# Reordered preparation, halved expert loads, single-chunk weight loads and later zeros in a two-layer gated cross-attention kernel

## The reference, cut to what matters

```python
x = x + jnp.tanh(g_xattn[0]) * _L0_xattn_ref(ctx_1024, _layernorm(x, axis=-1), mask, ...)   # 8 heads
x = x + jnp.tanh(g_ffn[0])   * _L0_ffn_ref(_layernorm(x, axis=-1), gate_w, w1, w2, w3)      # 8 experts, top 2
x = x + jnp.tanh(g_xattn[1]) * _L1_xattn_ref(ctx_1024, _layernorm(x, axis=-1), mask, ...)   # 16 heads
x = x + jnp.tanh(g_ffn[1])   * _L1_ffn_ref(_layernorm(x, axis=-1), w1, conv_w, conv_b, w2)

# in the cross-attention of layer A
x = layernorm(x, gamma_media, beta_media)               # the context
latents = layernorm(latents, gamma_lat, beta_lat)       # the tokens
kv = jnp.concatenate((x, latents * kv_gate), axis=1)
q, k, v = latents @ Wq, kv @ Wk, kv @ Wv                # masked softmax over k, then @ Wout
```

## Time and profile before

| | us |
|---|---|
| median of 3 runs | 1506.27 |
| the runs | 1496.41 to 1508.53 |
| the profiled execution | 1507.64 |
| its span, first to last instruction | 1505.9 |

### The profile page before, as it was taken

The page is one execution under the profiler, slowest core; times in us unless marked ns, Lnnn a source line. Parts: engine busy times, 40 slices in busy tenths (PEclk is TensorE's granted clock), DMA queues, the critical chain, the costliest instruction groups (busy, mean ns, idle before and its releaser), DMA issues.

```text
span 1505.9 us, 44898 instructions
## 1 busy us (share of the span) xinstructions
PE 1252.2 (83%) x16822; PEld 980.5 (65%) x16822; DVE 1075.0 (71%) x2786; ACT 973.2 (65%) x2319; POOL 1116.6 (74%) x1359
## 2 busy tenths in 40 slices
PE   1868787768769898977999999899999999999842
PEld 0545565547658776655887887677777777777631
DVE  4868786876555556775666766688888888888744
ACT  2868785555545576654655555687888887787731
POOL 5869787686566675547676777789889888988754
PEclk9989998889999999987999999999999999999965
DMA  7499999886999974547999999544655455454520
GB/s 223 98 232 229 230 241 221 166 219 148 242 179 249 235 171 91 93 101 181 236 229 252 247 256 241 107 106 97 104 97 105 104 108 104 95 110 102 78 41 6
DMA packets 439336, 239.94 MB, mean 159 GB/s; under 512 B 388960, under 2 KB 420560, under 8 KB 430544
## 3 DMA queue, kind: packets, MB, share of 16 engines
q1 hardware_dynamic: 407496, 172.87, 56.6%
q10 hardware_dynamic: 28552, 56.86, 12.4%
q0 software_dynamic: 3072, 7.34, 1.8%
HBM read 107.78 MB, written 35.50 MB: 95 GB/s over the span
## 4 chain that ended last, share of the span: by engine, by line
PE 32%; POOL 23%; DMA 13%; DVE 10%; issue 7%; ACT 6%; SPq 4%; DVEq 2%; ACTq 1%; POOLq 0%
PE bank_ring L1089 6%; DMA probs_turned<-probs 6%; POOL probs L651 6%; DMA expert_up<-experts_up 6%; PE bank_ring L1075 5%; PE bank_ring L1127 5%; PE bank_scores L1049 4%; PE bank_out L1108 3%; POOL raw_weights L696 3%; PE bank_x L1188 2%; ACT scores L852 2%; PE bank_x L1141 2%; POOL raw_weights L697 2%; POOL affine L627 2%; SPq L521 2%
## 5 line engine op out<-in xcount | busy, mean ns | idle before, releaser
L651 POOL TENSOR_TENSOR probs<-scores,probs 112x487 f16<-112x487 f32 x384 | 425.9, 1126 | 223.1 <-ACT probs L859 218.3
L852 ACT ACTIVATE scores<-scores,score_min 112x487 f32<-112x487 f32 x384 | 265.5, 693 | 81.8 <-DVE score_min L1340 79.5
L1340 DVE CUSTOM_DVE_ANT_0 scores<-bank_scores,mask 112x487 f32<-112x487 f32 x384 | 239.1, 660 | 48.9 <-PE bank_scores L1049 43.8
L859 ACT ACTIVATE probs<-scores 112x487 f16<-112x487 f32 x384 | 214.7, 604 | 37.0 <-DMA probs_turned<-probs 21.8
L1089 PE MATMUL bank_ring<-weights,kv_B 128*128 128x128 f16 x3072 | 196.8, 222 | 1.8 <-DVE keys L1352 1.8
L1089 PEld LDWEIGHTS bank_ring<-weights,kv_B 128*128 128x128 f16 x3072 | 185.8, 99 | 11.1 <-DVE keys L1352 2.5
L1108 PE MATMUL bank_out<-values,probs_turned 128*128 128x64 f16 x4608 | 171.3, 194 | 23.3 <-DMA probs_turned<-probs 22.7
L1357 DVE SCALAR_TENSOR_TENSOR values<-bank_ring,values 128x512 f16<-128x512 f32 x192 | 131.2, 683 | 80.4 <-ACT values L879 80.4
L879 ACT ACTIVATE values<-bank_ring 128x512 f16<-128x512 f32 x192 | 112.6, 587 | 110.5 <-PE bank_out L1108 109.1
L1075 PE MATMUL bank_ring<-kv_B,weights 128*128 128x488 f16 x768 | 181.1, 372 | 0.0
L1108 PEld LDWEIGHTS bank_out<-values,probs_turned 128*128 128x128 f16 x4608 | 158.6, 99 | 26.7 <-DMA probs_turned<-probs 13.0
(11 more groups left out here) (230 smaller groups left out, 2474.8 us busy)
## 6 DMA issues: line engine op xcount, KB each, us to landing
expert_up<-experts_up SPq DMA_DIRECT2D x43, 1024.0 KB, 5.3
expert_down<-experts_down SPq DMA_DIRECT2D x43, 512.0 KB, 6.8
raw_weights<-in_weights ACTq DMA_DIRECT2D x8, 1536.0 KB, 11.1
experts_up<-expert_up ACTq DMA_DIRECT2D x8, 1024.0 KB, 4.8
raw_weights<-in_weights ACTq DMA_DIRECT2D x6, 1024.0 KB, 8.3
probs_turned<-probs SPq DMA_TRANSPOSE x384, 3.3
context_turned_B<-kv_B ACTq DMA_DIRECT2D x16, 375.0 KB, 9.1
kv_B<-context_turned_B ACTq DMA_DIRECT2D x16, 375.0 KB, 3.7
```

What stands on the lines that cost most here:

```text
L651: pool.tensor_tensor(PR[:, u % 4, 1, 0:KEYS], S[:, u % 4, 0:KEYS], PR[:, u % 4, 0, 0:KEYS], ALU.subtract).then_inc(probs_split, 1)
L852: act_e.activation(S[:, u % 4, 0:KEYS], S[:, u % 4, 0:KEYS], ACT.Exp, bias=rmin[:, u % 4:u % 4 + 1], scale=-1.0, accum_out=rsum[:, g % 2, ...
L859: act_e.activation(PR[:, u % 4, 0, 0:KEYS], S[:, u % 4, 0:KEYS], ACT.Copy).then_inc(probs_ready, 1)
L1340: dve.tensor_tensor_reduce(out=S[:, u % 4, 0:KEYS], in0=bS[u % 2][0:TOK, 0:KEYS], in1=mask[:, m, 0:KEYS], scale=1.0, scalar=3.0e38, op0=AL ...
```

## The change

1. Mask and latents. `make_mask` is a function of its own with a semaphore `mask_made`; for layer A, POOL makes the mask first thing in step 4n - 4, ahead of the contexts, and SP loads the mask's bytes a step earlier. The queries' latents (two L627s, one L631) are split in step 4n - 5, and ACT rounds them there. Step 4n - 3 keeps the keys' latents alone. Layer B keeps its order.
2. `rstd`: the product and the sum with eps leave POOL; DVE does them in one `tensor_scalar` after a drain behind the statistics (two `tensor_scalar`s for stage P). POOL keeps the power.
3. Tiles' first matrices: `up` in DRAM and SBUF is laid out in two halves of 512 KB, each with semaphores. Half 0 of tile i + 2 is loaded between the two turns of step i, half 1 of tile i + 1 where all of it was before. A load needs only its own half of the buffer to be free.
4. Layer B's attention weights: one DMA of 256 KB in each of steps 37 to 52, four steps before ACT rounds the chunk.
5. Zeros: batch 0's five DMAs one in a step from 27; batch 1's seven one in a step from 58, out of `eup`, which DVE clears in step 57.
6. DVE's order: in a step without a tile, `early` parts (outputs and routing inputs) go before `split_expert` and the quantisation; in a step with a tile, before the quantisation too.
7. `combine` and `stats("B")` of sequences 0 and 6 go to the end of DVE's step 58 and 106.

```diff
-ZERO_STEP, ZERO_EACH = 27, 2
+ZERO_STEPS = (27, 58)
...
+def load_up(b, i, half):
...
+    e = sp.value_load(ids[b][0:1, i:i + 1], min_val=0, max_val=EXPERTS - 1)
+    if t >= 2:
+        sp.wait_ge(up_ready, 2 * (t - 2) + half + 1)
+    sp.dma_start(eup[:, t % 2, HALF_WORDS * half:HALF_WORDS * (half + 1)], up_dram[e, half])
...
     if 2 <= i + 1 < TILES[b]:
-        load_expert(b, i + 1, 0)
+        load_up(b, i + 1, 1)
     if 2 <= i < TILES[b]:
-        load_expert(b, i, 1)
+        load_down(b, i)
...
-    for u in (2 * j, 2 * j + 1):
-        turn_probs(u)
+    turn_probs(2 * j)
+    for b in range(2):
+        if 2 <= j - first_tile_step(b) + 2 < TILES[b]:
+            load_up(b, j - first_tile_step(b) + 2, 0)
+    turn_probs(2 * j + 1)
...
 def rstd(stage, n, cols):
-    after(pool.tensor_tensor(r[:, 0:cols], m[:, 0:cols, 1], growth[:, 0:cols], ALU.mult))
-    after(pool.tensor_tensor(r[:, 0:cols], r[:, 0:cols], bias[:, 0:cols], ALU.add))
     pool.tensor_tensor(r[:, 0:cols], r[:, 0:cols], minus_half[:, 0:cols], ALU.pow)
...
 if (j + 4) % 4 == 0 and 0 < (j + 4) // 4 < NSEQ:
+    make_mask(0, (j + 4) // 4).then_inc(mask_made, 1)
     split_context((j + 4) // 4, 0, 0)
...
+if (j + 5) % 4 == 0 and 0 < (j + 5) // 4 < NSEQ:
+    split_query_latents((j + 5) // 4)
...
-if j in (FFN_STEP + 5, FFN_STEP + 9):
-    load_raw(12 + i, i, 4, weights_in, L1_AT + 4 * i)
-if j in (L1_STEP + 5, L1_STEP + 9):
-    load_raw(14 + i, i, 4, weights_in, L1_AT + 8 + 4 * i)
+c = j - L1_STEP + 4
+if 0 <= c < L1_CHUNKS:
+    act_e.wait_ge(ffn_rounded if c < 8 else l1_split, c % 8 + 1)
+    act_e.dma_start(raw4(c), weights_in[:, (L1_AT + c) * CHUNK:(L1_AT + c + 1) * CHUNK])
...
 def up(b, i, half):
+    pe.wait_ge(up_loaded[t % 2][half], 16 * (t // 2 + 1))
     if half == 0:
-        pe.wait_ge(up_loaded[t % 2], 16 * (t // 2 + 1))
         pe.wait_ge(xt_loaded[t % 2], 16 * (t // 2 + 1))
...
 def stats(stage, n):
     dve.bn_stats(bn[0:TOK, at, :], X[:, n])
     dve.drain()
-    dve.bn_aggr(mv[stage][0:TOK, 0, :], bn[0:TOK, at, :]).then_inc(stats_ready[stage], 1)
+    dve.bn_aggr(mv[stage][0:TOK, 0, :], bn[0:TOK, at, :])
+    dve.drain()
+    dve.tensor_scalar(rs[stage][0:TOK, 0:1], mv[stage][0:TOK, 0, 1:2], 1.0 + LN_EPS, LN_EPS * LN_EPS,
+                      ALU.mult, ALU.add).then_inc(stats_ready[stage], 1)
...
+def clear_expert():
+    dve.wait_ge(up_ready, 2 * TILES[0])
+    dve.memset(eup[:, 0, 0:ZERO_ROWS * 2 * DIM], 0.0).then_inc(eup_cleared, 1)
...
     for n in range(NSEQ):
-        if j == combine_step(n):
+        if j == combine_step(n) and n not in FIRST_OF_BATCH:
             combine(n)
...
+    for n in FIRST_OF_BATCH:
+        if j == combine_step(n):
+            combine(n)
+            stats("B", n)
```

More of the change, by code:

```diff
@@ L1703, in _ @@
                         f_scale(n, 1)
+                if m[0]:
+                    for c in l1_chunk(j - 1):
+                        split_l1_chunk(c)
+                    gate_hidden(m[0][1], m[0][2], m[0][3])
+                for t in early(j):
+                    part(t)
                 for c in expert_chunks(j - 1):
```

183 lines of the change are left out of this document (103 added, 80 removed).

## The result

| | us |
|---|---|
| changed kernel, median of 20 runs | 1508.31 |
| the runs | 1500.74 to 1514.36 |
| kernel before beside it, median of 20 runs | 1498.77 |
| ratio | 1.0055, 95% interval 1.0031 to 1.0080 |
| profiled span, changed kernel | 1506.7 |

1467 us was forecast; the change made the kernel half a per cent slower. Medians further down are of all runs of a kernel; ratios leave out the runs in a slower state that some executions fall into.

What follows compares the result with a forecast made beforehand. PE's gaps in layer A (DMA share 0.99, no engine full) and the tiles were taken to count, with later layer B PE-bound. Terms -1 - 6 - 4 - 2.5 - 18 - 7 - 4 + 2 + 1 - 0.5 = -40 took 1507.6 to 1467 us; range 1445 to 1490.

Steps and rivals of the forecast that it cites:

- The mask, the latents and eps (-6 and -2.5): Layer A: keys ready up to 3.1 us sooner, 6 us gained (0 to 12); steps 33 to 38: 2.5 us (1 to 4).
- Batch 0 (-18): Steps 43, 47, 51, 55: PE's gaps at half 0 shrink through halves and single chunks, 18 us gained (9.8 to 28).
- rival D: Tiles: halves do nothing since the rows decide; batch 0 gives 6, batch 1 nothing, 1487 us, chance 0.07.
- Batch 1 (-7): Batch 1's tiles: halves take nearly all of 8.6 us of PE's waits, 7 us gained (3 to 8.5).
- zeros (-4 in steps 27 to 32): Steps 27 to 32: 3.2 of 5.6 MB of zeros leave a full DMA stretch, 4 us gained (0 to 8).
- step 106 (-3): Step 106: combination moved last puts DVE's work ahead of its wait for the gather, 3 us gained.
- Zeros in layer B (+1): Steps 58 to 64: the zeros return where transfers are about half, 1 us lost; 8 if turns get late.
- combination in step 58 (-1): Step 58: combination moved last, with PE already ahead, 1 us gained.
- rival C: Steps 58 to 64: later zeros hold up layer B's first turns, seven waits of 49 us in all, 1516 us, chance 0.04.
- Eps in layer B (+2): Layer B: DVE's added eps operation and drain lengthen ten statistics steps where PE waits, 2 us lost (0 to 4).
- A: Rival: DMA engines full in steps 6 to 32, so gaps move instead of going; 1486 us, chance 0.17.
- signs of being right: PE's `expert_up` waits under 10 us, POOL waits 10 to 14, steps 27 to 32 51 us, steps 64 to 192 outside tiles unchanged.

Runs made afterwards that it cites:

- e14: Changed kernel with POOL's split of the queries' latents in step 4n - 4, behind the first half of the context: 1489.88 us, 0.9894 of the kernel before.
- e2: Changed kernel with edit 1 alone undone: 1481.62 us, 0.9896 of the kernel before.
- e13: Kernel before with ACT's part of edit 1 alone (queries' latents rounded in step 4n - 5, ahead of the contexts): 1521.05 us, 1.0109.
- e8: Changed kernel without edits 1 and 4 (layer B's weights in four 1 MB loads again): 1494.84 us, 0.9950 of the kernel before.
- e9: Changed kernel without edits 1 and 3 (whole first matrices, single chunks kept): 1493.67 us, 0.9985 of the kernel before.
- the six and the fourteen: Six profiles of the kernel before, alone or with parts of edit 1, and fourteen of the changed kernel or variants; steps 39 to 56: medians 205.9 and 183.8 us.
- e6: Changed kernel without edits 1 and 7 (first combinations in their old place): 1496.70 us, 0.9895 of the kernel before.
- e5: Changed kernel without edit 1, with batch 1's zeros begun in step 60 instead of 58: 1483.81 us, 0.9839 of the kernel before.
- e11: Changed kernel without edits 1 and 2 (eps back on POOL): 1476.93 us, 0.9884 of the kernel before.
- e18: Changed kernel without edit 1, later zeros begun in step 60, in more rounds: 1476.66 us, 0.9829 of the kernel before.
- e4: Changed kernel with DVE's order in a step as before: 1503.57 us, 1.0030 of the kernel before.
- e10: Kernel before with edit 1 alone, but POOL's split of the queries' latents behind the second split of the probabilities: 1532.35 us, 1.0219.
- e17: Changed kernel without edit 1, with half of each 1.5 MB experts' load in steps 5 to 20 left out: 1474.59 us, 0.9796 of the kernel before.
- e16: Changed kernel with half of each 1.5 MB experts' load in steps 5 to 20 left out: 1490.05 us, 0.9917 of the kernel before.

## Why the prediction was wrong

**The mask, the latents and eps (-6 and -2.5): the step that failed.** The prediction put together what edit 1 takes "out of step 4n - 3 ahead of the mask's semaphore", and did not ask what the moved piece waits for at its new place nor what is queued behind it there. Its two L631 operations and L634 stand in step 4n - 5 ahead of both splits of the probabilities, and L634 waits for a rounding that ACT does after its work on the probabilities and the values. What was removed was seen rightly: PE's wait for POOL fell from 28.9 us to 12.0 in the changed kernel (9.9 for L658 and 2.1 for the mask, inside the forecast's 10 to 14). What the removal brought can't be told from nothing: e14 has the same fall without the new wait, and its ratio is e2's, with 11 us of room either way. The unseen wait of POOL for ACT, 65.0 us in 13 places, made edit 1 as a whole a loss of 1.6%, some 24 us, where a gain of 6 was put. In the same sum "0.85 us that ACT moves from its fullest step" was counted as a gain. On the kernel before it is a loss of 1.1% (e13). Why it costs there and not in e14 is open; the slow landings are the nearest thing to a reason that the traces show.

**Batch 0 (-18).** By the profiles 13.1 us in the changed kernel and 21.8 without edit 1, inside the bounds of 9.8 to 28. The split of the term was wrong. The prediction gave the halves alone 9.8 us as its lower bound and the chunks 6.5. The profiles give the halves alone 1.0 and the chunks alone 18.6 (they may be too large, as the ratios under e8 and e9 say). With the megabyte in flight the rows landed after 17.6 and 14.9 us, so rival D's mechanism, rows late ahead of `up`, was true wherever edit 4 is missing. A quarter of the megabyte did not leave a quarter of the difference: in step 46 of e9 the rows landed in 8.4 us, 10.2 less than in the earlier trace rows, where 5.9 was put, and in step 50 in 4.1, 3.4 less. The halves' 9.8 us took the rows' landings as given; without the chunks those of step 50 got later (14.9 us in e8). PE's gaps at half 0 in the changed kernel (its steps 43 and 47, had 6.30 and 13.84):

```profile
414.85 2.48 PE L1158 MATMUL bank_ring<-raw_weights,expert_up 128*128 128x128 f16 x24 [2.39 <-issue]
...
462.06 1.96 PE L1158 MATMUL bank_ring<-raw_weights,expert_up 128*128 128x128 f16 x24 [2.47 <-issue]
```

Both lie under the 4 to 6 us that the prediction left. Step 47 took 15.4 us at a granted clock of 0.89 (26.6 at 0.74 in the earlier trace rows). Its busy time stayed at 12.93, but for 159 matmuls and not 146: by these counts 0.081 us each instead of 0.087, against 0.074 in step 55 at 1.00, so a part of what the slow clock cost came back.

The Trainium skill (DMA: Bandwidth & Descriptors, Measured) would have DMAs batched to 1 MiB or more. Here the runs went the other way: sixteen chunks of 256 KB instead of four loads of 1 MB (e2 against e8) took 20.8 us off steps 39 to 56 by the profiles and about 8 us off the kernel by the ratios, though the median chunk took twice the 2.6 us that the page's fit (made on DMAs that GpSimd issues; these are ACT's) gives it as an estimate. In the changed kernel (DMA issues, KB each, median us to landing):

```profile
raw_weights<-in_weights ACTq DMA_DIRECT2D x16, 256.0 KB, 5.6
```

The page's rule is about one transfer's own bandwidth; what counted in this kernel was the small transfer behind it.

**Batch 1 (-7), zeros (-4 in steps 27 to 32), step 106 (-3).** By the two profiles -6.6, -5.4 and -3.9 for steps 104 to 107, by the medians of the six and the fourteen -5.6, -4.3 and -4.4. e9 gives the halves 6.1 us of batch 1, e6 gives edit 7 2.9 us in step 106: mechanism and size right. For the zeros the size fits, but no run leaves their spreading out, so the cause isn't shown; e5 to e9, e11 and e18, with the same zeros there, took 50.9 to 57.1 us.

**Zeros in layer B (+1), combination in step 58 (-1).** The sum for both was 0 and it was +5 in the profiles (e5: 4.3 us of step 58 come back). The prediction looked at the turns in steps 58 to 64 and at the load's average, and set its bound of 8 and its rival C by the turns. The transfer that PE had to wait for was another one, the gathers of step 58, issued 0.7 us ahead of the first 512 KB. These landed after 11.4 us in the changed kernel. The line that rival C named was wrong, its direction right.

**Eps in layer B (+2).** The stretch grew by 2.2 us, but e11 kept it with edit 2 undone, e4 with the old order and e6 without edit 7: the number fits and the reason doesn't. e8 and e9, without edits 4 and 3, kept it too (409.0 and 408.8). The growth itself is sure (the fourteen profiles lie over the six); which edit it is stays open.

**The rivals.** None of the five cases held. A says the DMA engines are full and gaps move. In the changed kernel PE's gap did move to the turns, but through a semaphore: e14 takes POOL's wait away, keeps every transfer, and gets the 1.6% back. That nothing was gained even so would fit A for edit 1's own term; it isn't shown. By A's own terms its sum comes to 22.8 us, not 22, which changes nothing. Without the two terms of edits 1 and 2 (8.5 us) the forecast's sum is 1507.6 - 31.5 = 1476, a ratio of 0.979; e18, without edit 1 and without the collision in step 58, measured 0.983 (0.979 to 0.987). Of the prediction's signs of being right three came true (no wait of PE for `expert_up` is left, 12.0 us for POOL, 49.9 us in steps 27 to 32), since none of them looks at what POOL waits for.

Of the 48 us between the forecast of -40 and the measured +8, edit 1 is 30 (-6 put, +24 measured). The other edits were put at -34 together and brought 16 by e2's ratio. The collision in step 58 is 5 of the missing 18; the rest lies in terms that one profile each can't size. A part of it may be that the forecast read its gaps from an execution 9 us above the median. The range and the chances held no case in which edit 1 itself loses, because the bounds of its term ran from 0 to 12.

## What to carry to other kernels

Before moving a piece of work to an earlier step of an in-order engine, look up what it waits for and when that is done in that step, and price everything that stands behind it; the saving at the old place is only half of the sum. When two edits clear the way for one wait, leave each out by itself: here, by the profiles, the smaller loads did nearly all of what the split matrices were credited with in batch 0. And a stretch of one profile is one execution: the ratio of many runs says how much of a row's gain is real. By e5, optional writes belong away from the step in which a small transfer on the path is issued, whatever the average load.

## What was not expected of the hardware

The same 1.5 MB load, in the same step and beside the same transfers, landed after 9.7 us in one execution and after 16.4 in another of the same code (step 8 of e2 and e5), and ACT's issue of a 375 KB DMA behind such a load lasted up to 11.08 us (e10), in which ACT did one operation and then stood for 8.7 us. Halving the loads brought 1.0 to 1.4% (e17 against e2, e16 against the changed kernel), though the DMA share hardly fell, from 0.96 to 0.90 and from 0.93 to 0.91.
